# Products with V in two blocks of eight key tiles, turned probabilities copied whole by ScalarE, and the chunk-end work in front of the turns

## The chip, the cores and the metric

The kernel runs on one core of one Trainium2 chip. The metric is the device time of one execution in microseconds. The median of three runs of the kernel before is 1283.56 us (1281.32 to 1284.36).

## The reference, cut to what matters

One transformer block in float32: attention, layer norm, a routed mixture of experts, layer norm.

```python
q, k, v = x @ Wq + bq, x @ Wk + bk, x @ Wv + bv      # x: 2048 x 512
# eight heads of 64 columns each, 2048 tokens
scores = einsum('bdsh,bdth->bdst', q, k) / sqrt(8)
feats = einsum('bdst,bdth->bdsh', softmax(scores), v)
x = layernorm(x + feats.reshape(B, S, F) @ Wo + bo)
# shared expert, and 64 routed experts of which each token takes 6 (capacity 256)
x = layernorm(x + shared(x) + routed(x))
```

## The kernel before, in words

The attention goes by chunks of 256 queries (NCH = 8 chunks) and within a chunk by heads (H = 8), so there are 64 heads in all, numbered m. A head has four steps u = 0 to 3. One loop variable s counts steps over all heads; every engine runs the same loop over s in its own instruction stream, and only semaphores tie them. The turns of a head lag its scores by LAG = 6 steps: at step s the step that is turned is r = s - 6, with m, u = divmod(r, 4).

For every head PE computes four score tiles of 128 queries by 1024 keys (score, L1683, six matmuls each, two row halves of the array side by side). VectorE takes each score tile out of PSUM, scales it and keeps the running minimum of the rows (L1364). ScalarE takes the exponential in place and sums the rows (L1018). PE turns the probabilities (turn_two, L1664: 32 transposes of 64x64 fill two PSUM slots of 128x1024, which stand for eight key tiles). The turned slots are copied into the tiles p_t: ScalarE copies the first half of each slot (L1004, two copies of 128x512), VectorE the second half (L1346, two copies of 128x512). Then PE multiplies by V (L1713, into the accumulator pv_acc). ScalarE reads pv_acc out into acc (L997), SyncE and GpSimd bring the two halves of acc together and scale them.

In PE's stream a head looks like this. At u = 0: turn_two, a small side step, two score tiles. At u = 1: nothing. At u = 2: turn_two, side step, two score tiles. At u = 3: all 16 key tiles of the product with V, for which PE waits for a_acc (the accumulator of the head before has been read out), a_pt and v_pt (the copies).

In ScalarE's stream: at u = 0 two copies of turned halves, then one exponential. At u = 1 first the read-out of pv_acc for the head before (L997), then an exponential. At u = 2 two copies and an exponential; at u = 3 an exponential. The read-out stands where `mj, uj = divmod(r - 2, STEPS)` gives uj = 3, which is u = 1 of the following head.

PSUM has three slots of two banks, taken in turn in the order that the list takes gives: turned, turned, scores, scores. A take waits until the take three before it has been read. So in each half head, the second score tile waits for the copy of the first turned slot; the second turned slot of the next half head waits for the minimum over the first score tile.

At the end of a chunk, side jobs are spread over the following steps (chunk_end in every engine's stream; side_step runs each job up to its next due tick, twice per step): two output projections (out_project, L1556), and for each of two row tiles the transposition of x1 (turn_x1, L1593), the gate scores (gate_scores, L1601) and the rank of each token within its expert (rank, L1611 and L1612). The first of the two side steps of a step stands between the turns and the scores. By the ticks, the first out_project falls before a product with V at u = 3, the second at u = 1, turn_x1 on an even step at u = 0, gate_scores at u = 1 (behind ScalarE's copy of the turned x1, L958), and rank behind the scores of u = 2.

Behind the attention come the shared expert, the 64 routed experts and the final sum; the change does not touch them.

Of the kernel before, what the change touches and what calls it, by code (L numbers as in the profile page):

```python
# [36 lines left out]
def build(nc, x, x_t, Wq, bq, Wk, bk, Wv, bv, Wo, bo, w_gate, w_sup, w_sdown, w_up, w_down, out):  # L37
# [9 lines left out]
    NT = T // P  # L47
# [11 lines left out]
    with ctx:  # L59
# [3 lines left out]
        def sem(name):  # L63
            return ctx.enter_context(nc.semaphore(name))
# [160 lines left out]
        a_x1t, a_score = sem("act_x1_turned"), sem("act_score")  # L225
        a_suphi, a_rhi, a_uphi, a_gate, a_y = (sem(f"act_{n}") for n in ("sup_hi", "rows_hi", "up_hi", "gate", "y"))
        v_xlo, v_wlo, v_klo, v_qlo, v_vadd = (sem(f"dve_{n}") for n in ("x_lo", "w_lo", "k_lo", "q_lo", "v_add"))
        v_min, v_pt, v_sum, v_inv = (sem(f"dve_{n}") for n in ("min", "p_turned", "sum", "inverse"))
        v_resid, v_norm = sem("dve_resid"), sem("dve_norm")
        v_meas, v_route = [sem(f"dve_measure{j}") for j in range(2)], [sem(f"dve_route{j}") for j in range(2)]  # L230
        v_suplo, v_rlo, v_gate, v_hid, v_base = (sem(f"dve_{n}") for n in (
# [64 lines left out]
        def slot_of_take(*take):  # L296
            return slots[place_of[take] % 3]

        def wait_bank(e, take, bank):

            if place_of[take] < 3:
                return
            kind, n = takes[place_of[take] - 3]
            if kind == "k":
                e.wait_ge(v_klo, 2 * n + 2)
            elif kind == "q":
                e.wait_ge(v_qlo, n + 1)
            elif kind == "v":
                e.wait_ge(v_vadd, n + 1)
            elif kind == "scores":  # L310
                e.wait_ge(v_min, n + 1)
            elif kind == "turn":
                e.wait_ge((a_pt, v_pt)[bank], n + 1)
            elif kind == "flip":
                e.wait_ge(v_rlo, n + 1)
            elif kind == "part":
                e.wait_ge(v_part, 2)
            elif kind == "up":
                e.wait_ge(v_hid, n + 1)
            elif n < SH or n >= NI:  # L320
                e.wait_ge(v_base, n + 1 if n < SH else n - E + 1)
            else:
                y_made(e, n - SH)
# [585 lines left out]
        def scalar(e):  # L909
# [79 lines left out]
            for s in range(LAST + LAG + 4):  # L989
                r = s - LAG  # L990
                m, u = divmod(r, STEPS)
                mj, uj = divmod(r - 2, STEPS)
                if mj >= 0 and uj == STEPS - 1:
                    e.wait_ge(p_pv, mj + 1)
                    if mj:
                        e.wait_ge(g_join, mj)
                    e.activation(acc[:, :], pv_acc[:, 0:QC], ACT.Copy).then_inc(a_acc, 1)  # L997
                if 0 <= r < LAST and r % 2 == 0:
                    if m >= 2:
                        e.wait_ge(p_pv, m - 1)  # L1000
                    for i in range(2):
                        view = slot_of_take("turn", r + i)[:, :].rearrange("p (t q) -> p t q", t=4)
                        e.wait_ge(p_turned[i], r + 1)
                        e.activation(p_t[m % 2][u + i][:, 0:2, :], view[:, 0:2, :], ACT.Copy).then_inc(a_pt, 1)  # L1004
                side_step(jobs)
                mv, uv = divmod(s - LAG - 1, STEPS)
                if mv >= 0 and uv == STEPS - 1 and mv % H == H - 1 and mv // H < END:
                    jobs.append(chunk_end(mv // H))
                if s == LAST + 4:
                    e.wait_ge(d_sup, 32)  # L1010
                    head_used(e, H - 1)
                    e.activation(sup_hi[:, :, :], sup_w[:, :, :], ACT.Copy).then_inc(a_suphi, 1)
                if 3 <= s < LAST + 3:
                    me, ue = divmod(s - 3, STEPS)
                    half, j = divmod(ue, QT)
                    e.wait_ge(v_min, 4 * me + 2 + j + 1)
                    keys = prob[:, me % 2, j, half * HALF:(half + 1) * HALF]
                    e.activation(keys, keys, ACT.Exp, bias=row_min[:, me % 2, j, 1:2], scale=-1.0,  # L1018
                                 accum_out=row_sum[:, me % 2, j, half:half + 1]).then_inc(a_exp, 1)
                side_step(jobs)  # L1020
# [93 lines left out]
        def vector(e):  # L1114
# [221 lines left out]
            for s in range(LAST + LAG + 4):  # L1336
                side_step(jobs)
                r = s - LAG
                m, u = divmod(r, STEPS)
                if 0 <= r < LAST and r % 2 == 0:  # L1340
                    if m >= 2:
                        e.wait_ge(p_pv, m - 1)
                    for i in range(2):
                        view = slot_of_take("turn", r + i)[:, :].rearrange("p (t q) -> p t q", t=4)
                        e.wait_ge(p_turned[i], r + 2)
                        e.tensor_copy(p_t[m % 2][u + i][:, 2:4, :], view[:, 2:4, :]).then_inc(v_pt, 1)  # L1346
                mv, uv = divmod(s - LAG - 1, STEPS)
                if mv >= 0 and uv == STEPS - 1 and mv % H == H - 1 and mv // H < END:
                    jobs.append(chunk_end(mv // H))
                if s == LAST + 5:  # L1350
                    e.wait_ge(a_suphi, 1)
                    e.tensor_tensor(sup_lo[:, :, :], sup_w[:, :, :], sup_hi[:, :, :].bitcast(F32),
                                    ALU.subtract).then_inc(v_suplo, 1)
                if s < LAST:
                    ms, us = divmod(s, STEPS)
                    half, j = divmod(us, QT)
                    e.wait_ge(p_scores, s + 1)
                    if ms >= 2:
                        for i in range(2):
                            e.wait_ge(p_turned[i], (ms - 2) * 4 + 2 * half + 2)  # L1360
                    if half:
                        e.wait_ge(v_min, s - 1)
                    first = row_min[:, ms % 2, j, 0:1] if half else 3.0e38
                    e.tensor_scalar(  # L1364
                        prob[:, ms % 2, j, half * HALF:(half + 1) * HALF], slot_of_take("scores", s)[:, :],
                        -1.0 / SCALE, first, ALU.mult, ALU.min,
                        accum_out=row_min[:, ms % 2, j, half:half + 1]).then_inc(v_min, 1)
                if s < V_LATE:
                    add_v(NS - V_LATE + s)
                if 0 <= r < LAST and u == 1:  # L1370
                    e.wait_ge(a_exp, 4 * m + 4)
                    if m:
                        e.wait_ge(d_inv, 16 * m)
                    e.tensor_tensor(row_inv[:, :], row_sum[:, m % 2, :, 0], row_sum[:, m % 2, :, 1],
                                    ALU.add).then_inc(v_sum, 1)
                    e.wait_ge(v_sum, m + 1)
                    e.reciprocal(row_inv[:, :], row_inv[:, :]).then_inc(v_inv, 1)
                side_step(jobs)
# [108 lines left out]
        def tensor(e):  # L1487
# [200 lines left out]
            for s in range(LAST + LAG + 4):  # L1688
                r = s - LAG
                m, u = divmod(r, STEPS)  # L1690
                if 0 <= r < LAST and r % 2 == 0:
                    turn_two(r)
                side_step(jobs)
                if s < LAST and s % 2 == 0:
                    score(s)
                    score(s + 1)
                    if s < V_LATE:
                        make_v(NS - V_LATE + s)
                        make_v(NS - V_LATE + s + 1)
                if s == LAST + 5:  # L1700
                    project_pairs(0)
                if 0 <= r < LAST and u == STEPS - 1:
                    if m == 0:
                        e.wait_ge(v_vadd, NS)
                    else:
                        e.wait_ge(a_acc, m)
                    for kt in range(NT):
                        if kt % 4 == 0:
                            e.wait_ge(a_pt, STEPS * m + kt // 4 + 1)
                        elif kt % 4 == 2:  # L1710
                            e.wait_ge(v_pt, STEPS * m + kt // 4 + 1)
                        half = slice(kt % 2 * D, (kt % 2 + 1) * D)
                        made = e.matmul(pv_acc[half, 0:QC], v_all[:, kt, m % H * D:(m % H + 1) * D],  # L1713
                                        p_t[m % 2][kt // 4][:, kt % 4, :], start=kt < 2, stop=kt >= NT - 2)
                    made.then_inc(p_pv, 1)
                mv, uv = divmod(s - LAG - 1, STEPS)
                if mv >= 0 and uv == STEPS - 1 and mv % H == H - 1 and mv // H < END:
                    jobs.append(chunk_end(mv // H))
                side_step(jobs)
# [158 lines left out]
```

## Time and profile before

| | before |
|---|---|
| median of three runs | 1283.56 us |
| the profiled execution's own time | 1283.6 us |
| its span in the trace | 1281.9 us |
| mean granted TensorE clock | 0.994 |
| attention loop, turns of the first head to turns of the 59th | 151.3 to 858.6 us |
| PE / VectorE / ScalarE busy | 91% / 68% / 55% |

The span is the time between the first and the last instruction. A busy PE in this table is time in which the trace shows a matmul under way. The mean of a group in the trace is the duration of one instruction, and idle time before it is charged to what released the engine.

### The profile page before, as it was taken

To read this page: it belongs to the slowest core of one execution; us is meant where nothing else is said; L and a number is where in the kernel's file an instruction comes from. 1 tells how busy PE (TensorE), PEld (TensorE's weight loads), DVE (VectorE), ACT (ScalarE), POOL (GpSimd) and SP (SyncE) were. 2 spreads that over 40 slices of the span, in tenths; PEclk is the share of its full clock that TensorE was granted. 3 is DMA by queue.
4 is the path that set the end of the run, shared out by engine and by line. 5 is a ranking of instruction groups with operands and counts; after the bars stand their busy time and mean duration, and the time that the engine had idled before them with its cause. 6 is when DMAs were issued, how large, how long until landed. Compare 5 with 4: busy or idle time off the path is not lost.

```text
span 1281.9 us, 28462 instructions
## 1 busy us (share of the span) xinstructions
PE 1169.5 (91%) x10564; PEld 813.9 (63%) x10564; DVE 869.0 (68%) x1693; ACT 707.9 (55%) x1243; POOL 380.8 (30%) x434
## 2 busy tenths in 40 slices
PE   7999988898898898898898998899898999999896
PEld 5888655556555556656656656656567788777642
DVE  5422566667767867868767767767776777776387
ACT  4320366655555655646556555655624788778343
POOL 0000011212422322321331331331442666667312
PEclk9999999999999999999999999999898999999999
DMA  8788445434544543553553544454688999997598
GB/s 285 252 295 280 134 136 143 150 111 132 134 101 100 146 127 80 152 137 77 147 129 90 154 125 94 140 170 114 203 298 332 381 390 382 345 334 252 227 423 342
DMA packets 105079, 257.88 MB, mean 201 GB/s; under 512 B 26904, under 2 KB 53464, under 8 KB 101616
## 3 DMA queue, kind: packets, MB, share of 16 engines
q1 hardware_dynamic: 84720, 201.25, 50.6%
q0 software_dynamic: 17920, 50.62, 10.3%
q10 hardware_dynamic: 2304, 4.20, 0.9%
q8 instruction: 87, 1.43, 0.5%
q14 instruction: 48, 0.39, 0.1%
HBM read 182.39 MB, written 134.98 MB: 248 GB/s over the span
## 4 chain that ended last, share of the span: by engine, by line
PE 69%; DVE 11%; issue 9%; ACT 6%; DMA 3%; POOL 1%; DVEq 0%; SPq 0%; ACTq 0%; POOLq 0%
PE pv_acc L1713 18%; PE slot L1493 11%; PE slot L1664 9%; PE slot L1683 5%; PE slot L1731 5%; PE slot L1779 5%; DVE prob L1364 5%; PE misc L1556 4%; ACT p_t L1004 4%; PE misc L1493 3%; PE pv_acc L1493 3%; DVE p_t L1346 2%; DMA got<-y_hbm 2%; ACT prob L1018 2%; PE slot L1821 2%
## 5 line engine op out<-in xcount | busy, mean ns | idle before, releaser
L1018 ACT ACTIVATE prob<-prob,row_min 128x1024 f32<-128x1024 f32 x256 | 293.1, 1150 | 63.1 <-DVE prob L1364 62.7
L1004 ACT ACTIVATE p_t<-slot 128x512 f32<-128x512 f32 x256 | 139.0, 595 | 299.3 <-PE slot L1664 298.6
L1346 DVE COPY p_t<-slot 128x512 f32<-128x512 f32 x256 | 164.6, 684 | 182.4 <-PE slot L1664 182.2
L1683 PE MATMUL slot<-k_rows,q_stack 64*128 64x512 f32 x1536 | 243.6, 419 | 33.7 <-ACT p_t L1004 14.6
L1713 PE MATMUL pv_acc<-p_t,v_all 128*64 128x256 f32 x2048 | 235.1, 382 | 0.0
L1664 PEld LDWEIGHTS slot<-ident,prob 64*128 64x128 f32 x4096 | 153.3, 139 | 95.4 <-issue 88.8
L1664 PE MATMUL slot<-ident,prob 64*128 64x64 f32 x4096 | 173.4, 228 | 43.6 <-DVE prob L1364 39.8
L857 POOL TENSOR_TENSOR moved<-acc,moved 64x256 f32<-64x256 f32 x63 | 46.0, 730 | 521.5 <-DMA moved<-acc 521.1
L1683 PEld LDWEIGHTS slot<-k_rows,q_stack 64*128 64x128 f32 x1536 | 139.7, 186 | 91.4 <-issue 85.1
L1713 PEld LDWEIGHTS pv_acc<-p_t,v_all 128*64 128x64 f32 x2048 | 141.4, 137 | 86.8 <-issue 21.4
L891 POOL DMA_INDIRECT y_hbm<-y_out,row_at x128 | 140.8, 1100 | 88.5 <-ACT y_out L1054 58.9
L1364 DVE TENSOR_SCALAR_CACHE_REDUCE prob<-slot,row_min 128x1024 f32<-128x1024 f32 x128 | 161.3, 1278 | 2.4
L1364 DVE TENSOR_SCALAR_CACHE_REDUCE prob<-slot 128x1024 f32<-128x1024 f32 x128 | 153.5, 1209 | 0.3 <-issue 0.3
L1395 DVE TENSOR_TENSOR rows_lo<-slot,rows_hi 128x1024 fp32r<-128x1024 f32 x69 | 84.3, 1223 | 56.7 <-ACT rows_hi L1030 55.7
L791 POOL DMA_INDIRECT disp_hbm<-resid,scat x84 | 83.8, 998 | 55.1 <-DVE scat L1264 34.5
L1054 ACT ACTIVATE y_out<-slot 128x1024 f32<-128x1024 f32 x64 | 62.2, 1024 | 44.6 <-PE slot L1779 44.6
L1731 PEld LDWEIGHTS slot<-ident,rows_all 128*128 128x128 f32 x576 | 65.5, 145 | 29.4 <-issue 24.6
L1731 PE MATMUL slot<-ident,rows_all 128*128 128x128 f32 x576 | 77.3, 280 | 4.0 <-DMA rows_all<-disp_hbm 3.9
L1030 ACT ACTIVATE rows_hi<-slot 128x1024 fp32r<-128x1024 f32 x69 | 70.7, 1025 | 15.3 <-PE slot L1731 15.3
L1779 PE MATMUL slot<-down_w,hid 64*128 64x512 f32 x256 | 64.9, 615 | 1.2 <-DVE hid L1422 1.2
L1493 PE MATMUL slot<-x_hi,w_hi 128*128 128x512 f32 x128 | 52.1, 407 | 6.9 <-DVE x_lo L1126 6.9
L1821 PE MATMUL slot<-got,rows_all 128*128 128x512 f32 x104 | 47.8, 599 | 5.7 <-DMA got<-y_hbm 3.0
(196 smaller groups left out, 1681.0 us busy)
## 6 DMA issues: line engine op xcount, KB each, us to landing
disp_hbm<-zero_hbm SPq DMA_DIRECT2D x64, 518.0 KB, 6.4
rows_all<-disp_hbm SPq DMA_DIRECT2D x64, 518.0 KB, 10.1
y_hbm<-zero_hbm SPq DMA_DIRECT2D x48, 512.0 KB
got<-y_hbm SPq DMA_DIRECT2D x15, 1536.0 KB, 19.9
q_stack<-q_hbm SPq DMA_DIRECT2D x128, 128.0 KB, 4.6
up_pair<-in_L_ffn_w_up SPq DMA_DIRECT2D x26, 512.0 KB, 7.4
down_w<-in_L_ffn_w_down SPq DMA_DIRECT2D x32, 256.0 KB, 10.4
q_hbm<-q_hi SPq DMA_DIRECT2D x8, 512.0 KB, 2.7
```

The lines of the kernel that those rows point to most:

```text
L891: e.indirect_dma_start(y_hbm, bass.IndirectOffsetOnAxis(row_at[:, 2 * g + t:2 * g + t + 1], 0), y_out[y][:, t, :], None, bounds_check=T * ...
L1004: e.activation(p_t[m % 2][u + i][:, 0:2, :], view[:, 0:2, :], ACT.Copy).then_inc(a_pt, 1)
L1018: e.activation(keys, keys, ACT.Exp, bias=row_min[:, me % 2, j, 1:2], scale=-1.0, accum_out=row_sum[:, me % 2, j, half:half + 1]).then_inc( ...
L1346: e.tensor_copy(p_t[m % 2][u + i][:, 2:4, :], view[:, 2:4, :]).then_inc(v_pt, 1)
L1364: e.tensor_scalar(prob[:, ms % 2, j, half * HALF:(half + 1) * HALF], slot_of_take("scores", s)[:, :], -1.0 / SCALE, first, ALU.mult, ALU.m ...
L1395: e.tensor_tensor(rows_lo[f % LEAD][:, :, :], slot_of_take("flip", f)[:, :].rearrange("p (k q) -> p k q", k=KC), rows_hi[f % LEAD][:, :, : ...
L1493: made = e.matmul(dst, weights[a](k), moving[b](k), start=(k, n) == (0, 0), stop=(k, n) == (KC - 1, 2))
L1664: made = e.transpose(views[i][:, t, j * P + side * D:j * P + (side + 1) * D], prob[rows_at, m % 2, j, (4 * (u + i) + t) * P:(4 * (u + i) + ...
L1683: made = e.matmul(slot[:, n * BANK:(n + 1) * BANK], qs[at, of_q, j * P:(j + 1) * P], keys[of_k], start=i == 0, stop=i == 2)
L1713: made = e.matmul(pv_acc[half, 0:QC], v_all[:, kt, m % H * D:(m % H + 1) * D], p_t[m % 2][kt // 4][:, kt % 4, :], start=kt < 2, stop=kt >= ...
L1731: made = e.transpose(view[:, k, t, :], rows[rows_of_item(f)][:, t, k * P:(k + 1) * P], ident[:, :])
L1779: made = e.matmul(slot_of_take("down", i)[:, t * BANK:(t + 1) * BANK], hid[pair % 2][at, t * P:(t + 1) * P], down_w[pair % ND][at, :], sta ...
```

## The change

Three edits, in the streams of ScalarE, VectorE and PE.

1. The turned slots are copied by ScalarE alone, one copy of 128x1024 for each slot in place of a half. It waits for the whole slot to be turned. VectorE's copies and its semaphore v_pt are gone.
2. The product with V is made in two blocks: at u = 1 the key tiles 0 to 7, at u = 3 the tiles 8 to 15. The wait for the read-out of the accumulator (a_acc) stands before the first block. ScalarE's read-out itself stays where it was in its stream.
3. PE's first side step of every step stands in front of the turns, no more between turns and scores.

```diff
@@ scalar, step loop
-                        e.wait_ge(p_turned[i], r + 1)
-                        e.activation(p_t[m % 2][u + i][:, 0:2, :], view[:, 0:2, :], ACT.Copy).then_inc(a_pt, 1)
+                        e.wait_ge(p_turned[i], r + 2)
+                        e.activation(p_t[m % 2][u + i][:, :, :], view[:, :, :], ACT.Copy).then_inc(a_pt, 1)
@@ vector, step loop
-                if 0 <= r < LAST and r % 2 == 0:
-                    if m >= 2:
-                        e.wait_ge(p_pv, m - 1)
-                    for i in range(2):
-                        view = slot_of_take("turn", r + i)[:, :].rearrange("p (t q) -> p t q", t=4)
-                        e.wait_ge(p_turned[i], r + 2)
-                        e.tensor_copy(p_t[m % 2][u + i][:, 2:4, :], view[:, 2:4, :]).then_inc(v_pt, 1)
@@ tensor, step loop
+                side_step(jobs)
                 if 0 <= r < LAST and r % 2 == 0:
                     turn_two(r)
-                side_step(jobs)
@@
-                if 0 <= r < LAST and u == STEPS - 1:
-                    if m == 0:
+                if 0 <= r < LAST and u % 2:
+                    if r == 1:
                         e.wait_ge(v_vadd, NS)
-                    else:
+                    elif u == 1:
                         e.wait_ge(a_acc, m)
-                    for kt in range(NT):
+                    for kt in range(4 * u - 4, 4 * u + 4):
                         if kt % 4 == 0:
                             e.wait_ge(a_pt, STEPS * m + kt // 4 + 1)
-                        elif kt % 4 == 2:
-                            e.wait_ge(v_pt, STEPS * m + kt // 4 + 1)
...
-                    made.then_inc(p_pv, 1)
+                    if u == STEPS - 1:
+                        made.then_inc(p_pv, 1)
```

wait_bank, through which PE reuses a slot, waits for a_pt alone in place of a_pt or v_pt by bank.

## Rows read from the trace of the kernel before

**Rows 1.** The page's busy times: us, share of the span, instructions.
```profile
PE 1169.5 (91%) x10564; PEld 813.9 (63%) x10564; DVE 869.0 (68%) x1693; ACT 707.9 (55%) x1243; POOL 380.8 (30%) x434
```

**Rows 2.** Windows: stretch, us, busy of each engine, PEclk, DMA share, GB/s.
```profile
151.30:239.09 87.79, 77.29 (x961) 52.60 (x962) 60.88 (x114) 57.25 (x105) 11.52 (x15) 1.00 0.48 138
363.68:462.93 99.25, 88.97 (x1008) 59.19 (x1006) 73.84 (x158) 57.71 (x108) 27.85 (x34) 1.00 0.47 119
...
759.71:858.62 98.91, 88.84 (x1007) 59.03 (x1006) 73.53 (x158) 57.71 (x108) 27.84 (x34) 1.00 0.44 120
```

**Rows 3.** Groups by line: busy, mean ns of one, idle before and releaser.
```profile
L1018 ACT ACTIVATE prob<-prob,row_min 128x1024 f32<-128x1024 f32 x256 | 293.1, 1150 | 63.1 <-DVE prob L1364 62.7
L1004 ACT ACTIVATE p_t<-slot 128x512 f32<-128x512 f32 x256 | 139.0, 595 | 299.3 <-PE slot L1664 298.6
L1346 DVE COPY p_t<-slot 128x512 f32<-128x512 f32 x256 | 164.6, 684 | 182.4 <-PE slot L1664 182.2
...
L1030 ACT ACTIVATE rows_hi<-slot 128x1024 fp32r<-128x1024 f32 x69 | 70.7, 1025 | 15.3 <-PE slot L1731 15.3
...
L997 ACT ACTIVATE acc<-pv_acc 128x256 f32<-128x256 f32 x64 | 24.6, 384 | 8.6 <-PE pv_acc L1713 8.6
```

**Rows 4.** Timeline of one head without side jobs: start, us, engine, group.
```profile
217.12 1.35 PE L1664 MATMUL slot<-ident,prob 64*128 64x64 f32 x32
...
218.32 1.09 ACT L1004 ACTIVATE p_t<-slot 128x512 f32<-128x512 f32 x2 [3.48 <-PE slot L1664]
218.58 1.29 DVE L1346 COPY p_t<-slot 128x512 f32<-128x512 f32 x2 [3.24 <-PE slot L1664]
219.29 1.15 ACT L1018 ACTIVATE prob<-prob,row_min 128x1024 f32<-128x1024 f32 x1
...
219.42 0.97 PE L1683 MATMUL slot<-k_rows,q_stack 64*128 64x512 f32 x6 [0.19 <-ACT p_t L1004]
...
220.43 0.38 ACT L997 ACTIVATE acc<-pv_acc 128x256 f32<-128x256 f32 x1
...
221.33 1.33 PE L1664 MATMUL slot<-ident,prob 64*128 64x64 f32 x32 [0.94 <-DVE prob L1364]
...
223.61 0.96 PE L1683 MATMUL slot<-k_rows,q_stack 64*128 64x512 f32 x6 [0.19 <-ACT p_t L1004]
...
224.50 3.67 PE L1713 MATMUL pv_acc<-p_t,v_all 128*64 128x256 f32 x32
...
228.11 1.10 PE L1664 MATMUL slot<-ident,prob 64*128 64x64 f32 x24
```

**Rows 5.** Timeline behind the attention: two ScalarE copies of 128x1024 out of PSUM.
```profile
941.06 1.94 ACT L1030 ACTIVATE rows_hi<-slot 128x1024 fp32r<-128x1024 f32 x2 [1.00 <-PE slot L1731]
```

**Rows 6.** Timeline of side jobs at a chunk's end.
```profile
851.38 3.70 PE L1556 MATMUL misc<-wo_sb,feats 128*128 128x512 f32 x8
...
873.54 0.66 PE L1593 MATMUL misc<-ident,resid 128*128 128x128 f32 x4
...
875.56 0.59 ACT L958 ACTIVATE x_t<-misc 128x512 f32<-128x512 f32 x1
...
876.21 1.10 PE L1601 MATMUL misc<-wg_sb,x_t 128*128 128x64 f32 x8 [0.42 <-ACT x_t L958]
```

**Rows 7.** Timeline of the last head's turns and product.
```profile
917.43 1.36 PE L1664 MATMUL slot<-ident,prob 64*128 64x64 f32 x32
...
920.99 1.74 PE L1664 MATMUL slot<-ident,prob 64*128 64x64 f32 x32 [2.21 <-ACT prob L1018]
...
924.73 4.63 PE L1573 MATMUL misc<-wo_sb,feats 128*128 128x512 f32 x6 [1.78 <-DVE x_t L1246]
...
932.90 1.12 PE L1578 MATMUL misc<-wo_sb,feats 64*128 64x512 f32 x2
```

**Rows 8.** Windows of PE at the last head: us, busy, PEclk, DMA share, GB/s.
```profile
920.00:925.00 5.00, 2.23 (x35) 0.66 0.88 247
```

More of the change, by code:

```diff
@@ L227, in build @@
         v_xlo, v_wlo, v_klo, v_qlo, v_vadd = (sem(f"dve_{n}") for n in ("x_lo", "w_lo", "k_lo", "q_lo", "v_add"))
-        v_min, v_pt, v_sum, v_inv = (sem(f"dve_{n}") for n in ("min", "p_turned", "sum", "inverse"))
+        v_min, v_sum, v_inv = (sem(f"dve_{n}") for n in ("min", "sum", "inverse"))
         v_resid, v_norm = sem("dve_resid"), sem("dve_norm")
@@ L312, in wait_bank @@
             elif kind == "turn":
-                e.wait_ge((a_pt, v_pt)[bank], n + 1)
+                e.wait_ge(a_pt, n + 1)
             elif kind == "flip":
```

## The prediction

> **What bounds the kernel now.** I read the busy times first [rows 1]: PE is busy 91% of the span, VectorE 68%, ScalarE 55%. So PE's stream is the path, and what counts is where it is held up. The windows say the same of the attention [rows 2]: eight heads without side jobs take 87.79 us, 10.97 a head, with PE busy for 77.29; eight heads with a chunk end take 98.91 (99.25 the longest; three more windows of that kind lie between 98.75 and 99.23). The clock is granted in full (1.00, the 2.4 GHz level) in all of them. Then I took the timeline of one plain head [rows 4], which repeats to 0.1 us in nearly all heads. The reader is to see two stretches in it, which I call A (turns of u = 0 to turns of u = 2: 217.12 to 221.33, 4.21 us) and B (turns of u = 2 to those of the next head: 221.33 to 228.11, 6.78 us); together 10.99. PE stands still 0.94 us in A ahead of the turns, because VectorE, which copies first (218.58, two copies, 1.29 us), takes the minimum late, and 0.19 us ahead of the second score tile in A and in B, for the copy of the first turned slot. B holds the whole product with V, 224.50 to 228.11, 3.61 us.
>
> **The change, step by step.** All times count from the start of the turns of that stretch.
>
> *Copies.* VectorE begins its copy, for which the whole slot must be turned, at 1.46 (218.58 - 217.12) [rows 4]. ScalarE gets that same wait, so I start its first whole copy there. It begins today at 1.20, on the half slot; this is the lower end. A whole copy is 128x1024: not in this place in the trace, but the row of the same engine, operation and size out of PSUM says 1025 ns [rows 3], and two of them back to back take 1.94 us [rows 5]. From below the cost is that of a copy that grows by its columns alone: 384 ns at 256 columns and 595 at 512 [rows 3] give 0.824 ns a column, so 595 + 422 = 1017 ns; from above it is two halves, 1190. I take 1025: same size, and near the lower end. First copy done at 2.485, both at 3.40. VectorE loses 164.6 us of work in all [rows 3], ScalarE gains 256 x (1025 - 595) ns = 110 us.
>
> *Second score tile.* It waits for the first turned slot. ScalarE's copy of the side job ends at 876.15 and PE's product starts at 876.21 [rows 6], so I add 0.06, and 0.03 from weight load to matmul (an estimate): start at 2.58. Today it is 2.30 (219.42). From this start to the product with V it is 0.89 (223.61 to 224.50) [rows 4]: PE is free for a block of eight at 3.47.
>
> *The 0.94 us in front of the turns* goes: VectorE has no copy before its minimum, and the block of eight stands between as well.
>
> *Block of eight at u = 1.* Half of 3.61 is 1.805. But in front of it stands the wait for a_acc: the read-out of the head before. ScalarE has that read-out at u = 1, behind two copies and an exponential. In rows 4 exactly this order is to be seen: copies 218.32, exponential 219.29, read-out 220.43 (the product it reads had ended before 217.2, over 3 us earlier). Until now nobody waited for it: the product came at u = 3. Now: copies done 3.40, exponential starts 0.12 before that (219.41 and 219.29), 3.28; read-out 1.14 later (220.43 - 219.29), 4.42; 0.384 long [rows 3], 4.80; PE sees it at 4.86. PE has been free since 3.47, so it stands 1.39 us in every head. Behind the waiting instruction are the block, the turns of u = 2 and all that follows on PE; SyncE's transfer of acc and GpSimd's join, which hang on the same read-out, come 1.1 us later than today (4.80 against 220.81 - 217.12 = 3.69), but are used more than a head later and cost nothing. A becomes 4.86 + 1.805 = 6.67.
>
> The Trainium skill ("PSUM — Partial Sum Buffer", section "Engine vs sequencer instructions") says that ScalarE's queue is strictly first in, first out; this speaks against the change, since the read-out can't pass the copies, and the order in rows 4 agrees. If it could pass them, the result would be that of rival 1.
>
> *Block of eight at u = 3.* Its copies are ready when the second score tile is over (the second copy at 3.40 + 0.06 is wanted for the fifth tile, later than 3.47). B becomes 3.47 + 1.805 = 5.28.
>
> *Is ScalarE itself late next?* In A it is busy from 1.46 to 5.9, in B from 1.46 to about 5.7 (two copies, two exponentials at 1.13 apart), then the next copies are due at 6.67 + 1.46 and 5.28 + 1.46. It isn't. The exponentials that the next head's turns want end about 0.8 us before these.
>
> *Plain heads.* A: +2.46 in 62 heads (not the first, which has no read-out to wait for, nor the last): +152.5. The first head's A is 5.28 against 4.12 to 4.21: +1.1. B: -1.50 in 62 heads: -93.0. Sum +60.6.
>
> *Chunk ends, seven in the loop.* Today they add 98.8 - 8 x 10.99 = 10.9 us to eight heads [rows 2]. Afterwards: the first out_project in B, 3.7 in full [rows 6]. The second in A, 3.47 + 3.7 + 1.8 = 8.98 against 6.67, +2.3: it fills the stall. turn_x1, now in front of the turns: 0.66 [rows 6] and no longer a cover for the copy; it wants the normalized rows, which VectorE makes behind the minimum over the last score tile, and I allow 0.3 for that (between 0 and 0.6; VectorE's minimum ends close to where B ends); twice 0.96, 1.9. gate_scores at u = 1: the copy of x1, 0.59 [rows 6], follows the exponential at 4.42, 5.01; the product 5.07 to 6.17, block to 7.98, +1.3, twice 2.6. rank: 0.15 each, an allowance that stands before and after. Sum 10.8; VectorE's routing, which today delays its copies and through them PE, is covered. Difference -0.1 each, -1 in all.
>
> *Last head.* No scores stand beside it. Today from its turns to the end of the product it is 917.43 to 932.90, 15.5 us, part of it at the lower clock (0.66 granted on average [rows 8], that is a mix of 1.2 and 2.4 GHz; the six matmuls of 924.73 take 4.63 [rows 7]), after PE stood 2.21 us and more. Afterwards A 6.67, turns 1.2, routing about 1, the six matmuls 2.3 to 4.6, block 1.8: 13.0 to 15.3. I take -1.5.
>
> Sum: +60.6 - 1 - 1.5 = +58. Against the profiled execution's own 1283.6 us (span 1281.9, 1.7 around it, 0.04 us from the median of the runs): **1341 us**.
>
> **Rivals.**
> 1. *The accumulator is read out before PE asks* (faster). Place: the read-out at L997; the point is 3.47 us after the turns. If it is over by then, with ScalarE ahead by 1.4 us there, A is 5.28 like B, a head takes 10.56, 0.43 less: -27. The side jobs cost slightly more, as they fill no stall (3.7 + 3.7 + 1.9 + 2 x 1.2 + 0.3 = 12.0 against 10.9, +8 over seven), the end gives -2: about 1262. For it: PE is the bound and gets rid of 0.94 us of stall. Against it: rows 4, where the read-out is the third thing that ScalarE does. Halving the copies' growth alone wouldn't do it: with today's 1.09 for both the read-out still ends at 3.95. 5%.
> 2. *The clock falls.* PE stands 1.39 us and 0.3 us in A, out of 6.67. Before the last head's second turns it stood 2.21 us and the granted clock fell to 0.66 [rows 7, 8]; with 0.94 in each head it stayed at 1.00 [rows 2]. Should each block behind the stall run at 1.2 GHz, that is 1.8 us more for each of 63 heads: +114, about 1455. 4%. The Trainium skill ("TensorE: Matmul & The Clock Gate", section "HAM oscillation — how this bites in real kernels") holds that stalls between groups of matmuls bring the half clock back; by that rule this rival would be likelier, and rows 2 with their 0.94 us stalls at 1.00 speak against it.
> 3. *The change doesn't relieve what it says*, VectorE's late minimum staying in front of the turns: PE would wait for it as now. But by rows 4 the minimum lasts 1.28 and would end at about 3.6, far ahead of 6.67. It would add nothing, and I give it nothing.
>
> **How the numbers follow.** Forecast 91%, rival 1 5%, rival 2 4%. The forecast's own uncertainty: copies starting at 1.20 and not 1.46 take 0.26 from A and B, -0.52 x 63 = -33; copies of 1.19 add 0.33 and 0.17, +31; the normalized rows +-4; the last head -2 to +1.5. These ends are unlikely together, so I go about half way to each: 1322 to 1358. That holds most of the forecast's 91%; rivals stay outside. A measurement of this kernel tells about 0.3% (4 us) from no change. Faster: rival 1, 0.05. Same: 0.01, between rival 1 and the forecast. Slower: 0.94.
>
> **What would show it.** In the timeline of a plain head: A about 6.7, B about 5.3; PE's first product with V idle before it some 1.4 us, released by ScalarE's read-out (L997 of before) in about 56 of 64 heads (elsewhere a side job stands there); no wait for the minimum in front of the turns; the second score tile waiting 0.45 to 0.5 us for the copy; copies of 128x1024 at 1.02 to 1.03 us; VectorE at about 705 us busy, ScalarE at about 818. Windows of eight plain heads at 95.6 us, with a chunk end at 106.4. The clock at 1.00. It is wrong if A is under 5.6 us, if the copies start much before 1.46, or if the windows show less than the full clock.

## The result, and the profile after

The changed kernel takes 1411.99 us in the median of four runs (1403.34 to 1415.3); the kernel before, in four runs, 1283.53 us. The ratio is 1.0995, with a 95% interval from 1.0969 to 1.1021. The forecast was 1341 us in a range of 1322 to 1358: the direction was right, the size was not. The loss is 128 us where 58 were forecast.

The profiled execution took 1403.34 us (span 1401.6), the fastest of the four. The busy times of its page (engine, us, share of the span) answer to [rows 1]: VectorE lost 151 us, ScalarE gained 102, and PE is busy for 56 us more than before with the same 10564 matmuls.

```profile
PE 1225.9 (87%) x10564; PEld 823.5 (59%) x10564; DVE 717.8 (51%) x1437; ACT 810.3 (58%) x1243; POOL 381.0 (27%) x434
```

The same number of matmuls in more busy time is the first sign that something other than a wait has been added. The groups by line (busy, mean ns of one, idle before and releaser; L1704 is the product with V, L1676 the scores) say where. The whole copy takes 1022 ns, as forecast from the 1025 of [rows 3]. The product with V has a mean of 439 ns, where that of the kernel before (its line L1713, shown first) was 382 for the same shape.

```profile
L1713 PE MATMUL pv_acc<-p_t,v_all 128*64 128x256 f32 x2048 | 235.1, 382 | 0.0
...
L1004 ACT ACTIVATE p_t<-slot 128x1024 f32<-128x1024 f32 x256 | 248.5, 1022 | 338.9 <-PE slot L1657 338.9
L1704 PE MATMUL pv_acc<-p_t,v_all 128*64 128x256 f32 x2048 | 296.0, 439 | 56.1 <-ACT acc L997 54.9
...
L1676 PE MATMUL slot<-k_rows,q_stack 64*128 64x512 f32 x1536 | 248.0, 420 | 64.5 <-ACT p_t L1004 64.2
```

The windows (stretch, us, busy of PE, PEld, DVE, ACT, POOL, granted clock, DMA share, GB/s) answer to [rows 2], where the clock was 1.00. Seven more windows of 100 us lie between 0.91 and 0.96.

```profile
151.30:250.00 98.70, 81.92 (x962) 52.93 (x960) 42.81 (x82) 69.62 (x105) 11.41 (x15) 0.97 0.46 124
250.00:350.00 100.00, 84.61 (x860) 52.72 (x856) 42.92 (x94) 58.16 (x91) 17.85 (x23) 0.91 0.35 105
```

The timeline of a plain head at full clock (start, us, engine, group), which answers to [rows 4]:

```profile
225.50 1.36 PE L1657 MATMUL slot<-ident,prob 64*128 64x64 f32 x32
...
226.96 1.94 ACT L1004 ACTIVATE p_t<-slot 128x1024 f32<-128x1024 f32 x2 [1.22 <-PE slot L1657]
...
228.12 0.97 PE L1676 MATMUL slot<-k_rows,q_stack 64*128 64x512 f32 x6 [0.51 <-ACT p_t L1004]
228.78 1.15 ACT L1018 ACTIVATE prob<-prob,row_min 128x1024 f32<-128x1024 f32 x1
...
229.91 0.38 ACT L997 ACTIVATE acc<-pv_acc 128x256 f32<-128x256 f32 x1
...
230.35 1.95 PE L1704 MATMUL pv_acc<-p_t,v_all 128*64 128x256 f32 x16 [1.26 <-ACT acc L997]
...
232.23 1.36 PE L1657 MATMUL slot<-ident,prob 64*128 64x64 f32 x32
```

Stretch A is 225.50 to 232.23, 6.73 us (forecast 6.67); B, 232.23 to 237.64 in the same trace, is 5.41 (forecast 5.28). The copies start 1.46 after the turns, the read-out is over at 4.79, and PE waits 1.26 for it: the walk came out nearly number by number. The reader should now look at another head, where the work is the same:

```profile
266.12 0.97 PE L1676 MATMUL slot<-k_rows,q_stack 64*128 64x512 f32 x6 [0.51 <-ACT p_t L1004]
268.34 3.26 PE L1704 MATMUL pv_acc<-p_t,v_all 128*64 128x256 f32 x16 [1.25 <-ACT acc L997]
271.53 1.64 PE L1657 MATMUL slot<-ident,prob 64*128 64x64 f32 x32
```

The same block of sixteen matmuls behind the same stall lasts 3.26 us and not 1.95, and A (263.49 to 271.53) is 8.04. Here the 1.2 GHz level was granted for most of the block. Of the 42 stretches A without a product of a side job, 23 are between 7.88 and 8.40 us; of the 14 with gate scores, 8 are between 9.41 and 9.66 where the others are 7.97 to 7.99. In each of these 31 the trace has a stretch at the 1.2 GHz level; the other stretches A before the last head have none. At a chunk's end two of the jobs that were priced look like this, turn_x1 first (it waits for the normalized rows) and then the gate scores (they wait for ScalarE's copy of the turned x1), with a block at the low clock behind them:

```profile
295.99 0.66 PE L1586 MATMUL misc<-ident,resid 128*128 128x128 f32 x4 [0.63 <-DVE resid L1203]
...
301.65 1.10 PE L1594 MATMUL misc<-wg_sb,x_t 128*128 128x64 f32 x8 [1.47 <-ACT x_t L958]
302.69 3.47 PE L1704 MATMUL pv_acc<-p_t,v_all 128*64 128x256 f32 x16
```

### The profile page after: what moved, and what is told of

The parts are those of the page before. It is cut to its first block, busy times and chain, and to the rows that moved or that the text cites. A ratio compares the mean times of both kernels' runs of the same rounds, so it can differ in the third digit from the quotient of the medians.

```text
span 1401.6 us, 28082 instructions
## 1 busy us (share of the span) xinstructions
PE 1225.9 (87%) x10564; PEld 823.5 (59%) x10564; DVE 717.8 (51%) x1437; ACT 810.3 (58%) x1243; POOL 381.0 (27%) x434
## 4 chain that ended last, share of the span: by engine, by line
PE 70%; ACT 16%; issue 6%; DVE 4%; DMA 3%; POOL 1%; SPq 0%; ACTq 0%; POOLq 0%; DVEq 0%
PE pv_acc L1704 19%; PE slot L1657 12%; PE slot L1486 10%; ACT p_t L1004 9%; PE slot L1676 5%; ACT prob L1018 5%; PE slot L1771 4%; PE slot L1723 4%; PE misc L1549 4%; PE pv_acc L1486 3%; PE misc L1486 3%; DMA got<-y_hbm 2%; PE slot L1813 1%; PE misc L1594 1%; ACT acc L997 1%
## 5 line engine op out<-in xcount | busy, mean ns | idle before, releaser
L1004 ACT ACTIVATE p_t<-slot 128x1024 f32<-128x1024 f32 x256 | 248.5, 1022 | 338.9 <-PE slot L1657 338.9
L1704 PE MATMUL pv_acc<-p_t,v_all 128*64 128x256 f32 x2048 | 296.0, 439 | 56.1 <-ACT acc L997 54.9
L1676 PE MATMUL slot<-k_rows,q_stack 64*128 64x512 f32 x1536 | 248.0, 420 | 64.5 <-ACT p_t L1004 64.2
L1704 PEld LDWEIGHTS pv_acc<-p_t,v_all 128*64 128x64 f32 x2048 | 153.2, 153 | 176.9 <-ACT acc L997 73.0
L1357 DVE TENSOR_SCALAR_CACHE_REDUCE prob<-slot,row_min 128x1024 f32<-128x1024 f32 x128 | 164.1, 1283 | 154.4 <-PE slot L1676 153.2
L1676 PEld LDWEIGHTS slot<-k_rows,q_stack 64*128 64x128 f32 x1536 | 140.5, 186 | 121.1 <-issue 116.6
L1657 PE MATMUL slot<-ident,prob 64*128 64x64 f32 x4096 | 178.5, 232 | 1.7 <-ACT prob L1018 1.5
L1549 PE MATMUL misc<-wo_sb,feats 128*128 128x512 f32 x112 | 51.8, 605 | 0.0
```

The lines of the kernel that those rows point to most:

```text
L1004: e.activation(p_t[m % 2][u + i][:, :, :], view[:, :, :], ACT.Copy).then_inc(a_pt, 1)
L1357: e.tensor_scalar(prob[:, ms % 2, j, half * HALF:(half + 1) * HALF], slot_of_take("scores", s)[:, :], -1.0 / SCALE, first, ALU.mult, ALU.m ...
L1549: made = e.matmul(bank_of(c, j)[:, :], feats_of(c)[:, k, j * P:(j + 1) * P], wo_sb[:, k, :], start=k == 0, stop=k == KC - 1)
L1657: made = e.transpose(views[i][:, t, j * P + side * D:j * P + (side + 1) * D], prob[rows_at, m % 2, j, (4 * (u + i) + t) * P:(4 * (u + i) + ...
L1676: made = e.matmul(slot[:, n * BANK:(n + 1) * BANK], qs[at, of_q, j * P:(j + 1) * P], keys[of_k], start=i == 0, stop=i == 2)
```

## The experiments

Theory 1: the loss has two parts, PE's stall for the read-out (about 1.25 us a head), and the half clock that this standing still brings to the block behind it. Theory 2: the clock falls for another reason, the whole copies, through their two shorter waits in each head or the memory they share with PE.

**The read-out in front of the copies.** In ScalarE's stream of the changed kernel:

```diff
-                mj, uj = divmod(r - 2, STEPS)
+                mj, uj = divmod(r - 1, STEPS)
```

> The changed kernel with one edit: ScalarE's read-out of the accumulator stands in front of the copies of u = 0, so it is done about 0.7 us after the turns begin and PE has nothing to wait for at u = 1. Theory 1 (the read-out stall costs 1.25 us a head, and it is this stall that takes the clock to half for the block behind it): stretch A falls from 6.73 to about 5.4 like B, the granted clock goes back to nearly 1.00 outside the heads with gate scores, 1300 to 1320 us. Theory 2 (the clock falls because PE is idler overall, two waits of 0.52 us a head for the whole copies): A falls too, but the windows keep a granted clock of 0.91 to 0.97, about 1345 us.

Measured: 1313.27 us, ratio to the kernel before 1.0243 (1.0226 to 1.026): 99 us less than the changed kernel, by a line that moves one copy of 0.38 us. A is 5.40 in nearly all plain heads, like B. Windows of PE (us, busy, clock, DMA share, GB/s), first heads and the first chunk end:

```profile
151.00:250.00 99.00, 90.02 (x1118) 1.00 0.51 144
250.00:350.00 100.00, 88.36 (x950) 0.97 0.39 116
```

Theory 1 holds. The waits of 0.51 us for the whole copies are all still there, and alone they leave the clock at 1.00. What is left of the low clock (windows at 0.97 to 0.98) stands in nine of the fourteen heads with gate scores, where PE still waits 1.47 us for ScalarE's copy of the turned x1: A is up to 10.57 there, and none of the plain stretches A is at the low clock.

**The stall filled with work of no use.** Changed kernel, five products more before the wait, in the heads in which no side job used the bank of misc (reads is the length of misc_read at the start of the step). Their result is read by nobody, and the rest is computed as before.

```diff
+                        if len(misc_read) == reads:
+                            wait_misc()
+                            e.wait_ge(a_pt, STEPS * m + 1)
+                        for i in range(5 if len(misc_read) == reads else 0):
+                            half = slice(i % 2 * D, (i % 2 + 1) * D)
+                            e.matmul(misc[half, 0:QC], v_all[:, i % 4, 0:D], p_t[m % 2][0][:, i % 4, :],
+                                     start=True, stop=True)
                         e.wait_ge(a_acc, m)
```

> The changed kernel with five products more (as those with V, 0.23 us each at full clock, into a PSUM bank nobody reads then) in front of the wait for the read-out at u = 1, in the heads in which no side job used that bank. The stall is filled with work of no use, nothing else changes. Theory 1: A stays at 6.73 in the heads at full clock, the heads at 7.9 to 8.4 fall to it, granted clock 1.00 in windows without gate scores; about 1365 us. Theory 2: the clock falls all the same, in part because of the copy waits; 1400 us or more.

Measured: 1364.79 us, ratio 1.0647 (1.0629 to 1.0665). With 210 products more (each stands as two matmul instructions, 10984 against 10564) the kernel is 47 us faster. A is 6.67 to 6.79 in the plain heads, but for one of 7.01 and the first head, which has no read-out to wait for (5.31). The low clock is left in eight heads with gate scores, which the fill doesn't reach. This parts the loss: the half clock that the fill can reach costs 47 us; the stall, the longer path and the half clock left in those eight heads cost the other 81.

```profile
151.00:250.00 99.00, 90.54 (x1076) 1.00 0.44 132
250.00:350.00 100.00, 89.27 (x950) 0.98 0.38 112
```

**The blocks of eight alone.** The kernel before with edit 2 only; the copies stay shared between ScalarE and VectorE, and the product keeps its waits for v_pt.

```diff
-                if 0 <= r < LAST and u == STEPS - 1:
+                if 0 <= r < LAST and u % 2:
...
-                    for kt in range(NT):
+                    for kt in range(4 * u - 4, 4 * u + 4):
```

> The kernel before with the blocks of eight alone (copies shared with VectorE, side step behind the turns as before). Theory 1: the read-out ends at about 3.7 us after the turns, PE is free at 3.2, so a stall of 0.56 us is left, A about 5.6, B about 5.1, a head 10.7; full clock; about 1255 us, faster than before. Rival (cutting the product in two costs by itself, or the read-out wait in any size brings the clock down): 1285 us or more, with a granted clock under 0.99.

Measured: 1256.65 us, ratio 0.979 (0.9774 to 0.9806). The blocks are a gain of 27 us when ScalarE's copies are short. In the timeline the read-out now starts 3.31 us after the turns (225.73), where it started at 4.41 with whole copies, and PE waits 0.46 us for it; A is 5.62, B 5.08, the clock 1.00 in all windows up to 850 us.

```profile
225.73 1.37 PE L1664 MATMUL slot<-ident,prob 64*128 64x64 f32 x32
...
229.04 0.38 ACT L997 ACTIVATE acc<-pv_acc 128x256 f32<-128x256 f32 x1
229.47 1.95 PE L1713 MATMUL pv_acc<-p_t,v_all 128*64 128x256 f32 x16 [0.46 <-ACT acc L997]
...
231.35 1.36 PE L1664 MATMUL slot<-ident,prob 64*128 64x64 f32 x32
```

**The whole copies alone.** The kernel before with edit 1 only, all sixteen tiles at u = 3.

```diff
-                        e.wait_ge(p_turned[i], r + 1)
-                        e.activation(p_t[m % 2][u + i][:, 0:2, :], view[:, 0:2, :], ACT.Copy).then_inc(a_pt, 1)
+                        e.wait_ge(p_turned[i], r + 2)
+                        e.activation(p_t[m % 2][u + i][:, :, :], view[:, :, :], ACT.Copy).then_inc(a_pt, 1)
```

> The kernel before with the whole copies by ScalarE alone (all 16 key tiles at u = 3, side step behind the turns as before). Theory 1: the copy wait grows by 0.33 us in A and in B, but VectorE's minimum is early and most of the 0.94 us in front of the turns goes; A 3.7, B 7.15, a head 10.8; full clock; about 1262 us. Theory 2 (the whole copies and their waits are what brings the clock down): granted clock under 0.97 and over 1300 us.

Measured: 1340.19 us, ratio 1.044 (1.042 to 1.0459); my number was 78 us off. I had overlooked a wait: the turns of u = 2 also need the exponential that ScalarE makes behind its two copies, and with whole copies it is late. PE waits 1.06 us for it in front of the turns, more than the 0.94 of [rows 4] that were to go. A is 4.66, B 7.10, and B is 7.8 to 8.2 in a third of the heads: here too the clock falls.

```profile
567.97 0.97 PE L1676 MATMUL slot<-k_rows,q_stack 64*128 64x512 f32 x6 [0.51 <-ACT p_t L1004]
...
570.00 1.33 PE L1657 MATMUL slot<-ident,prob 64*128 64x64 f32 x32 [1.06 <-ACT prob L1018]
```

**That wait filled.** The kernel above with four products of no use at u = 1. First on a chip on which the kernel before itself took 1307.78 us:

```diff
+                if 1 < r < LAST and u == 1 and len(misc_read) == reads:
+                    wait_misc()
+                    e.wait_ge(a_pt, STEPS * m + 1)
+                    for i in range(4):
+                        half = slice(i % 2 * D, (i % 2 + 1) * D)
+                        e.matmul(misc[half, 0:QC], v_all[:, i % 4, 0:D], p_t[m % 2][0][:, i % 4, :],
+                                 start=True, stop=True)
```

> The kernel with the whole copies alone, and four products more of no use at u = 1, in the 1.06 us in which PE waited for ScalarE's exponential, in the heads where no side job used that bank. Theory 1 (idle time of PE inside a head brings the clock down, whatever it waits for): A stays 4.67, the stretches B of 7.8 to 8.0 fall to 7.1, granted clock 0.98 or more, 1318 to 1325 us against 1340 without the added work. Theory 2 (the whole copies slow the products by themselves, through the memory that both use): no change, 1340 us.

Measured: 1362.93 us, ratio 1.0418 (1.0378 to 1.0459), not to be told from 1.044 on another chip. So both were run once more, side by side on one chip where the kernel before took 1283.21:

> The kernel with the whole copies alone once more, for a comparison on one chip with the filled one. Both theories: 1.04 of the kernel before, granted clock about 0.965.

> The same with four products of no use in the 1.06 us wait at u = 1. Theory 1 (idle time of PE brings the clock down): 15 to 22 us less than without them, granted clock 0.98 or more. Theory 2 (the whole copies slow the products by themselves): within 4 us of it.

Measured: 1337.11 us (1.0431, 1.0415 to 1.0447) without the added work, 1329.63 us (1.0359, 1.0344 to 1.0374) with it. The added work takes off 7.5 us, and the granted clock rises from 0.971 to 0.983. The sign is theory 1's, the size half of what I expected. The traces show why. Of the stretches B without an output projection, 18 are of 7.7 us and over without the added work. Nine of them start with the wait of 1.06 to 1.08 us, and all nine are gone with it: before the last head, no head that got the added work has the low clock. The other nine stand in heads with gate scores, where it has no place and PE stands 1.47 us for ScalarE's copy of the turned x1; there the added work leaves nine as well (nine of fourteen heads in both runs, not the same ones). Nine stretches that are some 0.75 us shorter (7.84 to 7.10) make 7 us. I had expected the gate heads to gain too.

**The side step alone, and the side step undone.** Both on the chip of 1307.78 us, so only ratios count.

```diff
+                side_step(jobs)
                 if 0 <= r < LAST and r % 2 == 0:
                     turn_two(r)
-                side_step(jobs)
```

> The kernel before with the side step in front of the turns alone. Theory 1 (the moved job is turn_x1 alone, 14 times, 0.6 us of PE that no longer lies beside a copy, and the gate scores find the same wait for ScalarE): about +0.6 us each, 1290 us, full clock. Rival (it costs nothing, as its place was on the path before too): 1283 us.

> The changed kernel with the side step back behind the turns. Theory 1: the 14 stretches B that end with turn_x1 fall from 6.70 to 5.4 (0.66 of product and 0.63 of wait for the normalized rows), the gate heads keep their wait for ScalarE and their half clock: about 1394 us. Rival (the moved side work is a larger part of the loss, through the clock): under 1380 us.

Measured: the edit alone on the kernel before 1.0058 (1.0028 to 1.0087), a loss of 7.6 us (7 expected); the changed kernel without it 1.0778 (1.0735 to 1.082) in place of 1.0995. That is 2.2 points, 28 us at 1283, where 18 were expected, but the two ratios come from different chips, and the times themselves (1413.08 and 1411.99) don't differ. The traces give the part that doesn't hang on the chip: in the changed kernel the 14 stretches B that end with turn_x1 are 5.98 to 7.06 where others are 5.41, 14 us together, and without the edit no such stretch is left, while the heads with gate scores keep their 7.97. Of more than these 14 us nothing is shown.

**The read-out in front and the copies shared.** The blocks alone with the read-out moved as in the first experiment.

> The kernel before with the blocks of eight and the read-out in front of the copies of u = 0 (copies shared, side step behind the turns). Theory 1: the stall of 0.5 us that the blocks alone still have goes in the heads without a side job at u = 1; A and B 5.07, full clock, about 1232 us, the fastest so far. Rival (the read-out delays the copies, or the stall comes back in front of another instruction): 1250 us or more.

Measured on the chip of 1307.78 us: 1284.25, ratio 0.9817 (0.9787 to 0.9847). In that trace PE stood still within a run of transposes, with nothing in the profile that it waited for ("remote" is what the view names where it knows no releaser), while GpSimd sent scatters and SyncE transfers:

```profile
304.99 0.46 PE L1664 MATMUL slot<-ident,prob 64*128 64x64 f32 x8 [1.24 <-remote]
```

This trace has 22 such stops of over 0.2 us, up to 2.37, 22 us in all. Runs on the other chips, the kernel before among them, have none within a run of transposes.

Once more, beside a variant, where the kernel before took 1283.21 us:

> Blocks of eight with the read-out in front of the copies once more. Theory 1: on a chip on which the kernel before takes 1283 us it takes 1232 us, a ratio of 0.96, as A falls from 5.6 to 5.1 in some 45 heads against the blocks alone (0.979). Rival (the read-out's place is worth nothing once the copies are shared): 0.979 again.

> The same with the gate scores one side step later, behind the block of eight, so that PE does not stand for ScalarE's copy of the turned x1. Theory 1: 14 times 0.1 to 0.2 us, 1230 us, 0 to 3 us under the one before. Rival (ScalarE, which then waits for the gate scores, comes late to the next copies): 1235 us or more.

The variant's edit is in PE's chunk_end:

```diff
-                    yield from to(start + 3)
+                    yield from to(start + 4)
                     gate_scores(c, j)
```

Measured: 1243.47 us (0.9692, 0.9679 to 0.9704) and 1241.25 us (0.9672, 0.9649 to 0.9696). Both beat the kernel before, the second by 42 us, and the blocks alone by 13 to 15 (another chip, on which the kernel before took the same 1283 us); between the two there is no difference that could be told. The 1232 expected were not reached. Plain heads are 5.08 + 5.08 as computed, but a few stretches A in each of the two, among heads 4 to 8 above all, are 5.5 to 6.8, and one is 8.91. In the timeline of the second kernel:

```profile
192.58 2.89 SPq L593 DMA_DIRECT2D disp_hbm<-zero_hbm  x2
...
195.57 0.54 SPq L684 DMA_DIRECT2D moved<-acc  x1
...
202.52 0.73 POOL L857 TENSOR_TENSOR moved<-acc,moved 64x256 f32<-64x256 f32 x1 [9.50 <-DMA moved<-acc]
...
203.34 0.38 ACT L997 ACTIVATE acc<-pv_acc 128x256 f32<-128x256 f32 x1 [2.75 <-POOL moved L857]
203.62 1.08 ACT L1004 ACTIVATE p_t<-slot 128x512 f32<-128x512 f32 x2
...
204.31 0.97 PE L1683 MATMUL slot<-k_rows,q_stack 64*128 64x512 f32 x6 [1.02 <-ACT p_t L1004]
```

The read-out in its new place overwrites acc, so it must wait until GpSimd has joined the one before. The join waits for SyncE's transfer (moved<-acc), which SyncE issues behind two transfers of zeros (192.58); here the join starts 6.95 us after that issue. With the copies queued behind the read-out, PE pays 1.02 us. From the issue of this transfer to the join it is 5.3 us in the median of this trace and 2.2 in the kernel before, where ScalarE's read-out never waits for GpSimd. Which part of the longer way is the zeros' and which other traffic's is not shown.

## Why the prediction was wrong

**Right by its own steps.** The copies' start (1.46 forecast, 1.46 measured), their cost (1.025, 1.022), the order in which ScalarE reaches the read-out and the stall that follows (1.39 from when PE is free, 1.26 measured as idle time), the end of the 0.94 us in front of the turns, the longer A and shorter B: all as written. The first experiment shows the stall as the cause of the larger part, with the low clock that it brings: without it 99 of the 128 us are gone.

**Wrong: the step that failed is rival 2.** I gave the fall of the clock 4%, as a thing that happens to all blocks (+114) or to none, and put it aside by the row that 0.94 us of stall had left it at 1.00 [rows 2]. It happened to about half of them: in the profiled execution 23 plain heads lose 1.2 to 1.7 us each (34 us), 8 gate heads some 1.5 each (12 us), a number of stretches B the rest, 50 us together. That execution was the fastest of the four, at a granted clock of 0.959; in the others (0.949 to 0.955) the loss by the clock is larger, about 59 us in the median (an estimate: the span times the share of the clock that is missing, less the same in the kernel before). The fill experiment gives 47 us of it back and leaves the gate heads. The row I went by was one stall of 0.94 and two of 0.19 in a head of 11 us; the changed kernel has one of 1.26 and two of 0.51, and rows 7 and 8, with 2.21 us and a clock of 0.66, lay on the other side. Between the two I had no row, and should have carried the half clock as an unknown cost with both ends, 0 and +114, in the range. The Trainium skill ("TensorE: Matmul & The Clock Gate", section "HAM oscillation — how this bites in real kernels") tells of a kernel in which waits for DMA of 3 to 5 us between groups of matmuls bring back the half clock, group after group. These runs agree that stalls between groups can bring it back, and show it with stalls of 1.06 to 1.47 us, shorter than the page's, a difference that the prediction left out: a fill of no use took 47 us off, and with the fill the windows are at 0.97 to 1.00.

**Under-sized terms at full clock.** With the half clock taken out, about 70 us of the profiled execution's 120 are left, against 58. A block of eight takes 1.87 to 1.88 us to the next turns and not half of 3.61 (+0.07, 126 times, 9 us). In B the block starts 3.53 us after the turns and not 3.47 (+0.06, 63 times, 4 us), as the second score tile starts later. From the last head's turns to the end of its product it is 15.2 us, 0.3 less than before and not 1.5 less (+1 us): PE stands 3.49 us for the read-out there. Together that is 14, against the 12 that are missing. The chunk ends were priced right: turn_x1 costs 14 us in all against 13 (it waits 0.63 to 1.00 for the normalized rows in seven of the 14 places and 0.13 or nothing in the others, where 0.3 was allowed for each), and a gate head at full clock 1.24 against 1.3 (7.97 - 6.73).

**Wait overlooked without harm.** The forecast named the exponentials that the next head's turns want, and not the one of the turns of u = 2. In the changed kernel the read-out stall covers it. With the whole copies alone it is the stall, and my expectation there failed by it.

**Rival 1**, the read-out done before PE asks, did not come true in the changed kernel. Made true by an edit, with whole copies, it gives 1313 and not 1262. Estimates from its trace come to about the 51 us between them: a plain head is 5.40 + 5.40 and not 10.56 (15 us), A with gate scores is 7.97 and not 6.5, since PE waits for ScalarE there (14 times, 21 us), and the low clock in nine of these heads and the stretches behind them costs about 17 (0.981 against 0.994 granted).

## What to carry to other kernels

When work is moved forward on the engine that is the bound, look at every other engine's stream for what that work waits for, and move the producer with it: here one read-out of 0.38 us, left where it stood, was worth 99 us. Splitting the product in two paid here where the copies in front of it stayed short, shared between two engines (27 us, and 40 to 42 with the read-out moved); with whole copies, and the side step in front of the turns, it lost 30 us even with the read-out moved. And a new stall on PE of the size seen here (1.06 to 1.47 us in a head) belongs in the sum twice, once as time and once as clock, or is tried with work of no use in the gap.

## What was not expected of the hardware

- Adding 210 products (0.23 us each at full clock) made the kernel 47 us faster, since the blocks behind them ran at 2.4 GHz (block 1.95 us in place of up to 3.63).
- The granted clock did not fall with waits of 0.51 us twice a head (1.00 over 99 us), nor with 0.94 and two of 0.19 [rows 2]; it fell in about half of the heads with 1.26 and two of 0.51, in eight to ten of the 14 with 1.47 for the gate scores, and in about a third with 1.06 and two of 0.51. Why one head and not the next, with the same work, stays open.
- The kernel before took 1283 us in three sessions, on two chips at least, and 1307.78 us (1303.81 to 1314.56, eleven runs) on another chip. In all four traces of kernels run there (the kernel before is not among them) PE stops within runs of transposes, by up to 2.37 us and for 7 to 22 us in all; no trace from the other chips has such a stop of over 0.2 us. No run here shows what it stood for, or whether it is the whole difference.
